# Edge convolution of a graph network: rows gathered two turns ahead, four one-hot slots, four rotating PSUM banks, transposes one group later, node state kept in DRAM

## What is computed

```python
x = norm(x + two hops of normalized neighbour sums of x)
x = norm(x + conv2(leaky_relu(conv1(x))))
x = norm(x + sixteen hops with alpha = 0.1)
x = norm(x + gcn(relu(graph_norm(gcn(x)))))

def _egnn_conv(x, src, dst, edge_attr, W_msg, W_edge, W_root, b):
    msg = x[src] @ W_msg + edge_attr @ W_edge
    agg = jax.ops.segment_max(msg, dst, num_segments=x.shape[0])
    agg = jnp.where(jnp.isneginf(agg), 0.0, agg)
    return agg + x @ W_root + b
```

## Time and profile before

| | us |
|---|---|
| three runs: lowest, median, highest | 2440.36, 2442.22, 2445.31 |
| the profiled execution | 2427.74 |
| its span, first to last instruction | 2425.9 |
| busy: PE, DVE, POOL, ACT | 1989.3, 1248.0, 717.9, 637.2 |
| convolution turns, start of turn 0 to start of turn 25 | 457.52 and 457.16 |
| mean granted clock of PE | 0.931 |

### The profile page before, as it was taken

One profiled execution on the slowest core, in us unless ns is written; L12 is line 12 of the kernel. 1 busy time (PEld: TensorE's weight loads), 2 busy tenths in 40 slices (PEclk: granted clock), 3 DMA queues, 4 the chain that ended last, 5 costly groups with the idle time before them and its releaser, 6 DMA issues. The chain is left out here.

```text
span 2425.9 us, 55088 instructions
## 1 busy us (share of the span) xinstructions
PE 1989.3 (82%) x22874; PEld 1903.6 (78%) x22874; DVE 1248.0 (51%) x3350; ACT 637.2 (26%) x1659; POOL 717.9 (30%) x681
## 2 busy tenths in 40 slices
PE   4587468888888358888888369999999999999877
PEld 3587467787777357877877259999999999999767
DVE  7934446666656336666656454444444444445435
ACT  5832212212211112112112123323333333332231
POOL 4512146656656535566655510000000000000000
PEclk9988789999999679999999679999999999999879
DMA  2023236656655336566656300000000000000000
GB/s 71 1 82 103 83 80 137 136 128 137 137 122 136 92 78 131 125 138 139 132 129 134 94 6 2 2 2 2 2 1 2 2 2 2 2 2 2 3 3 21
DMA packets 223177, 157.62 MB, mean 65 GB/s; under 512 B 147494, under 2 KB 208581, under 8 KB 222679
## 3 DMA queue, kind: packets, MB, share of 16 engines
q1 hardware_dynamic: 90841, 80.91, 12.9%
q0 software_dynamic: 22064, 32.18, 7.9%
q10 hardware_dynamic: 110024, 41.02, 6.2%
HBM read 99.40 MB, written 54.55 MB: 63 GB/s over the span
## 5 line engine op out<-in xcount | busy, mean ns | idle before, releaser
L757 PE MATMUL l_ps<-l_u,counts 125*128 125x192 f16 x11250 | 940.4, 247 | 77.8 <-DVE l_u L800 65.1
L757 PEld LDWEIGHTS l_ps<-l_u,counts 125*128 125x128 f16 x11250 | 935.3, 98 | 82.9 <-issue 64.8
L1119 PE MATMUL c_taken<-y,c_hot 125*128 125x192 f16 x6500 | 601.6, 252 | 174.4 <-issue 74.8
L1119 PEld LDWEIGHTS c_taken<-y,c_hot 125*128 125x128 f16 x6500 | 551.5, 100 | 206.9 <-issue 86.9
L1089 POOL DMA_INDIRECT c_gathered<-messages,idx_all x572 | 567.8, 993 | 397.4 <-PE c_msg L1109 246.1
L1167 DVE TENSOR_SCALAR c_hot<-c_offset_srcs 125x640 f16<-125x640 f16 x1300 | 339.6, 327 | 262.7 <-PE c_taken L1119 187.7
L1177 DVE TENSOR_TENSOR_SCAN c_scanned<-c_mask,c_scanned,c_msg 96x512 f32<-96x512 bf16 x208 | 264.2, 1270 | 127.9 <-remote 101.9
L820 DVE SCALAR_TENSOR_TENSOR l_uf<-l_ps,l_cf,l_wide 125x96 f32<-125x96 f32 x400 | 127.2, 318 | 329.1 <-ACT l_wide L776 329.1
L1231 ACT ACTIVATE c_back<-c_tr 128x384 f32<-128x384 f32 x208 | 103.1, 496 | 625.9 <-PE c_tr L1129 361.9
L776 ACT ACTIVATE l_wide<-l_ps,l_cl 125x96 f32<-125x96 f32 x400 | 136.0, 341 | 306.8 <-PE l_ps L757 306.8
L782 ACT ACTIVATE l_u<-l_uf 125x96 f16<-125x96 f32 x400 | 113.2, 283 | 265.3 <-DVE l_uf L824 254.3
(11 more groups left out here) (236 smaller groups left out, 1143.9 us busy)
## 6 DMA issues: line engine op xcount, KB each, us to landing
running_max<-c_back ACTq DMA_DIRECT2D x208, 192.0 KB
c_attr<-attr_halves SPq DMA_DIRECT2D x412, 64.0 KB
c_mask<-segment_mask SPq DMA_DIRECT2D x206, 96.0 KB
c_gathered<-messages,idx_all POOLq DMA_INDIRECT x572
c_srcs<-sources SPq DMA_DIRECT2D x50, 156.2 KB
l0a_raw<-in_ea_t SPq DMA_DIRECT2D x25, 265.6 KB
attr_halves<-l0a_hi SPq DMA_DIRECT2D x25, 132.8 KB
attr_halves<-l0a_lo SPq DMA_DIRECT2D x25, 132.8 KB
```

Source lines behind the costliest of these rows:

```text
L757: last = pe.matmul(ps[:, t % HB, 0:2 * F], at[:, k, t * P:t * P + 128], u[hop % 2][:, k, :], start=(k == 0), stop=(k == T - 1))
L1119: last = pe.matmul(acc[:, j // 2, j % 2 * (2 * F):(j % 2 + 1) * (2 * F)], hot[:, h % 2 * HALF + k, j * ET:(j + 1) * ET], y[:, t, :], start ...
```

## The change

1. **Gathered rows double-buffered.** `gathered` holds 11 tiles for each of two turns; the taken tiles have their own buffer. POOL's gathers for turn i wait for the messages of turn i-2; those of turns 0 and 1 wait for nothing.
2. **Four one-hot slots.** Eight chunks of 3 blocks (the last has 4) in four slots. DVE refills a slot after the chunk four earlier.
3. **Four rotating banks** for the takes. Turn i uses banks 3i, 3i+1, 3i+2 modulo 4. ACT evacuates and signals each bank on its own; the first and the last chunk of a turn go bank by bank.
4. **Turn-back one group later.** PE: messages 0; chunks 0, 1; turn-back 3 of turn i-1; messages 1; chunks 2, 3; turn-back 0; messages 2; chunks 4, 5; turn-back 1; messages 3; chunks 6, 7; turn-back 2. `evacuate` comes before `send_back` 2 on ACT.
5. **State parked in DRAM.** SP stores `x_state` to `xs_d` at the end of the first two hops, and the next stage begins when the store has landed; SBUF is then free for the buffers above. `conv_result` loads it back, behind the root term on SP's queue, and DVE waits for it before its first use.
6. **Layout of `scan_d`.** Four tiles of a row side by side: stores of 1536 bytes in place of 4 x 384. `end_idx` is worked out for that by seven small DVE operations on 125 x 25 elements, at the start of the first convolution (`ends=True`).
7. `keys`, the hops' `u0` and the rows `y` share one buffer, and sources are loaded a turn earlier.

The diff, cut to what the text speaks of:

```diff
-CHUNKS = (range(0, 5), range(5, 9), range(9, 13), range(13, 17), range(17, 21), range(21, 25))
+CHUNKS = tuple(range(3 * h, 3 * h + 3) for h in range(7)) + (range(21, 25),)
 NC = len(CHUNKS)
-RING = 2 * max(len(r) for r in CHUNKS)
+SLOTS = (0, 3, 6, 9)
+RING = 13
+ACCS = 4
...
+        y = rows16[0:P, :, :]
+        with ExitStack() as s1:
+            xs = s1.enter_context(nc.sbuf_tensor("x_state", [P, T, F], F32))
+            build_counts(ctx, src, dst, xs, x)
+            with ExitStack() as st:
+                hs = hop_state(ctx, st, "l0", teleports=False)
+                hops(ctx, "l0", hs, xs, 1.0, 0.0, 2, norm=xs, out=xs_d, halves=AttrHalves(ctx, st, "l0a"))
+            node_product(ctx, "c1w", xs, "W1_msg", "W1_root", "b1", y16=y)
...
+        edge_conv(ctx, "c1", "W1_edge", y, ends=True)
...
+        edge_conv(ctx, "c2", "W2_edge", y)
+        xs = keep("x_state_back", [P, T, F], F32)
         with ExitStack() as st:
             c2 = st.enter_context(nc.sbuf_tensor("c2", [P, T, F], F32))
-            conv_result(ctx, "c2r", c2, xs)
+            conv_result(ctx, "c2r", c2, xs, xs_d)
...
-        gat = sb("gathered", [ET, IT, 2 * F], F16)
+        gat = sb("gathered", [ET, 2, FROM_POOL, 2 * F], F16)
+        tak = sb("evacuated", [ET, TAKEN, 2 * F], F16)
...
-        acc = st.enter_context(nc.psum_tensor(f"{tag}_taken", [128, NB, BANK], F32))
+        acc = st.enter_context(nc.psum_tensor(f"{tag}_taken", [128, ACCS, BANK], F32))
...
-        scan_v = c["scan_d"].rearrange("(g j p) f -> g p j f", j=GT, p=ET)
+        s_ch = sem(f"{tag}_ch")
+        scan_v = c["scan_d"].rearrange("(g p j) f -> g p j f", j=GT, p=ET)
...
+                load_srcs(1, TE)
                 for i in range(N_IT):
-                    if i < last_it:
-                        load_srcs(i + 1, LEFT_TAKEN if i + 1 == last_it else TE)
+                    if i + 2 < N_IT:
+                        load_srcs(i + 2, LEFT_TAKEN if i + 2 == last_it else TE)
...
                 for i in range(N_IT):
                     for g, tiles in enumerate(by_dma):
-                        pool.wait_ge(s_msg, i * GT + g + 1)
+                        if i >= 2:
+                            pool.wait_ge(s_msg, (i - 1) * GT + g + 1)
                         for j in tiles:
                             pool.indirect_dma_start(
-                                out=gat[:, j, :], out_offset=None, in_=c["y_d"],
+                                out=gat[:, i % 2, j, :], out_offset=None, in_=c["y_d"],
                                 in_offset=bass.IndirectOffsetOnAxis(ap=idx_all[:, i * IT + j:i * IT + j + 1], axis=0),
-                            ).then_inc(s_gat[g], 16)
+                            ).then_inc(s_gat[i % 2][g], 16)
...
                 def take(i, h):
-                    if h == 0:
-                        pe.wait_ge(s_evac, i + 1)
                     pe.wait_ge(s_hot, i * NC + h + 1)
-                    for k, t in enumerate(CHUNKS[h]):
-                        for j in range(TAKEN):
-                            last = pe.matmul(acc[:, j // 2, j % 2 * (2 * F):(j % 2 + 1) * (2 * F)],
-                                             hot[:, h % 2 * HALF + k, j * ET:(j + 1) * ET], y[:, t, :],
-                                             start=(t == 0 and j % 2 == 0), stop=(t == T - 1), skip_group_check=True)
-                    last.then_inc(s_took, 1)
+                    chunk = CHUNKS[h]
+                    slot = SLOTS[h % len(SLOTS)]
+                    def one(k, j):
+                        t = chunk[k]
+                        return pe.matmul(acc[:, (NB * i + j // 2) % ACCS, j % 2 * (2 * F):(j % 2 + 1) * (2 * F)],
+                                         hot[:, slot + k, j * ET:(j + 1) * ET], y[:, t, :],
+                                         start=(t == 0 and j % 2 == 0), stop=(t == T - 1), skip_group_check=True)
+                    if 0 < h < NC - 1:
+                        for k in range(len(chunk)):
+                            for j in range(TAKEN):
+                                last = one(k, j)
+                    else:
+                        for b in range(NB):
+                            if h == 0 and b == 0 and i >= 2:
+                                pe.wait_ge(s_evac, NB * (i - 1))
+                            if h == 0 and b > 0 and i >= 1:
+                                pe.wait_ge(s_evac, NB * (i - 1) + b)
+                            for j in range(2 * b, min(2 * b + 2, TAKEN)):
+                                for k in range(len(chunk)):
+                                    last = one(k, j)
+                            if h == NC - 1:
+                                last.then_inc(s_pair, 1)
+                    if h < NC - 1:
+                        last.then_inc(s_took, 1)
...
-                def body(i, more):
+                def takes(i, *chunks):
+                    if i < N_IT:
+                        for h in chunks:
+                            take(i, h)
+                pe.wait_ge(s_we, 2)
+                takes(0, *range(NC))
+                for i in range(N_IT):
                     messages(i, 0)
-                    if more:
-                        take(i + 1, 0)
-                        take(i + 1, 1)
+                    takes(i + 1, 0, 1)
+                    if i:
+                        turn_back(i - 1, 3)
                     messages(i, 1)
+                    takes(i + 1, 2, 3)
                     turn_back(i, 0)
-                    if more:
-                        take(i + 1, 2)
-                        take(i + 1, 3)
                     messages(i, 2)
+                    takes(i + 1, 4, 5)
                     turn_back(i, 1)
                     messages(i, 3)
-                    if more:
-                        take(i + 1, 4)
+                    takes(i + 1, 6, 7)
                     turn_back(i, 2)
-                    if more:
-                        take(i + 1, 5)
-                    turn_back(i, 3)
-                pe.wait_ge(s_we, 2)
-                pe.sem_inc(s_evac, 1)
-                for h in range(NC):
-                    take(0, h)
-                for i in range(N_IT):
-                    body(i, i < last_it)
+                turn_back(last_it, 3)
...
+                def one_hots(i, *chunks):
+                    for h in chunks if i < N_IT else ():
+                        v.wait_ge(s_off, i + 2)
+                        if h >= len(SLOTS):
+                            v.wait_ge(s_took, i * (NC - 1) + h - len(SLOTS) + 1)
+                        elif i and h < len(SLOTS) - 1:
+                            v.wait_ge(s_took, (i - 1) * (NC - 1) + h + len(SLOTS) + 1)
+                        elif i:
+                            v.wait_ge(s_pair, i * NB)
+                        for k, t in enumerate(CHUNKS[h]):
+                            last = v.tensor_scalar(hot[:, SLOTS[h % len(SLOTS)] + k, :], off[:, :], float(t * P - SRC_MID), None, ALU.is_equal)
+                        last.then_inc(s_hot, 1)
...
+                if ends:
+                    ch = Chain(v, s_ch)
...
+                    v.scalar_tensor_tensor(c["end_idx"][:, :], tile, 1.0 - GW, end, ALU.mult, ALU.add)
...
+                one_hots(0, *range(NC))
+                one_hots(1, 0, 1, 2, 3)
                 for i in range(N_IT):
-                    body(i, i < last_it, i < last_it - 1)
+                    scan(i, 0)
+                    one_hots(i + 1, 4, 5)
+                    scan(i, 1)
+                    one_hots(i + 1, 6, 7)
+                    scan(i, 2)
+                    one_hots(i + 2, 0, 1)
+                    scan(i, 3)
+                    one_hots(i + 2, 2, 3)
...
-                    act.wait_ge(s_took, i * NC + NC)
                     act.wait_ge(s_msg, i * GT + GT)
                     for b in range(NB):
                         n = min(2, TAKEN - 2 * b)
-                        last = act.activation(gat[:, FROM_POOL + 2 * b:FROM_POOL + 2 * b + n, :],
-                                              acc[:, b, 0:n * 2 * F].rearrange("p (j f) -> p j f", f=2 * F), ACT.Copy)
-                    last.then_inc(s_evac, 1)
+                        act.wait_ge(s_pair, NB * i + b + 1)
+                        act.activation(tak[:, 2 * b:2 * b + n, :],
+                                       acc[:, (NB * i + b) % ACCS, 0:n * 2 * F].rearrange("p (j f) -> p j f", f=2 * F),
+                                       ACT.Copy).then_inc(s_evac, 1)
...
+                    if i:
+                        send_back(i - 1, 3)
+                    send_back(i, 0)
+                    if i + 2 < N_IT:
+                        act.wait_ge(s_hot, (i + 2) * NC)
+                        offset_srcs(i + 2)
+                    send_back(i, 1)
+                    if i < last_it:
+                        evacuate(i + 1)
+                    send_back(i, 2)
+                send_back(last_it, 3)
...
                 conv.sync(sp)
```

(3 more changed lines are left out.)

105 lines of the change are left out of this document (34 added, 71 removed).

## The result

| | before | after |
|---|---|---|
| median of the runs, us | 2441.29 (2439.29 to 2445.31, 4 runs) | 2548.03 (2537.39 to 2551.9, 4 runs) |
| the profiled execution | 2427.74 | 2548.67 |
| its span | 2425.9 | 2546.8 |
| busy PE, DVE, POOL, ACT | 1989.3, 1248.0, 717.9, 637.2 | 2052.4, 1257.9, 711.0, 645.0 |

The ratio is 1.0428, with an interval of 1.0394 to 1.0462. The forecast was 2499 us, in a range of 2360 to 2560, with 0.67 for slower. The direction and the place were right; the turns cost far more than I said, and so did the parking.

A forecast was written before the change was run, and what follows sets the result against it. PE bounds the hops; in turns, its signals are also held during POOL's back-to-back gathers. Starts +28.6, turns +25, parking +10.5 and tail -7 took 2427.7 to 2484.8; 14.5 more for the median gave 2499 us, range 2360 to 2560.

The forecast's parts named there:

- What bounds the kernel: In turns, PE's 14.4 us of work in 18.3, with the rest lost to the evacuation wait and the hold.
- The hold: While POOL issues gathers back to back, PE's signals from about 2 us in wait until about 1 us after.
- A, the starts: Start of each convolution: 22 gathers in one run instead of 11, 14.3 us later each, +28.6 in all.
- B, the turns: 50 turns: evacuation wait goes, PE halts earlier in gather runs, more runs merge; +25 us, bounds -100 to +60.
- The merged runs: Turns where POOL runs through two groups' gathers: one in seven or so costs 3.5 us more, +0.5 a turn.
- The plain turn: Turn with gather runs of 4, 4, 3: 14.4 work + 3.4 + 0.5 halts = 18.3 us, as before.
- C, the parking: Store ending the first hops +3.5 us, fetch behind the root term in conv_result +7; together +10.5.
- D: Small parts (index operations, longer store packets, evacuate order, earlier sources, shared buffers): 0 us, bounds 0 to 3.
- E: Tail: the last two turns of each convolution have no gathers beside them, -3.5 us each, -7 in all.
- Double-buffering pays: Rival in the turns: PE still meets four-gather runs late, turn 16.3 us, 2374 us in all; chance 0.15.
- PE gets further: Rival in the turns: PE runs 32 takes further past a held signal, turn near 15.9, 2354 us; chance 0.10.

The follow-up runs named there:

- gated run: Changed kernel with POOL's waits as before the change (gathers wait for the previous turn's messages), undoing double-buffering alone; 2520.53 us (one run).
- the parking in the better order: Changed kernel, SP storing four fifths of the state before the last attribute halves and fetching root term and state fifth by fifth; 2534.99 us (one run).

## Why the prediction was right, and where it was short

**What bounds the kernel: right.** The hold decides the sign. It goes with the spacing of the gathers: the table above has a border between 1.4 and 1.50 us in the quiet start and between 1.50 and 1.57 in the turns. That fits the 1.44 a gather, read from one idle time of DVE, as the rate at which a backlog goes; the backlog itself is not seen.

**A, the starts: right.** +13.4 and +13.0 against 14.3 each. The gated run gives it back, and more.

**B, the turns: right in kind, short by 51 us** (+69 with the tail against +18). The 48 turns with gathers grew by 76 us, which lies outside B's own bound of +60, and the turn is 19.6 and 19.8 on average where I had given 18 to 19. The whole stayed in the range all the same, as it had been drawn wide. Three things in it:

- The merged runs. I took one turn in seven, each 3.5 us above a plain turn of 18.3; one in three merged, which I had as the bound. They took 21.55, 3.25 above 18.3, so the price was about right and the number was not: 16 x 3.25 = 52 us instead of 25.
- The plain turn. It took 19.07 instead of 18.3: 32 x 0.77 = 25 us. **The term that was mis-sized is PE's 14.4 us of work, not its halts.** In the 19 plain turns at full clock PE is busy for 15.4 and idle for 3.55, where I had 14.4 and 3.9; before, plain turns at full clock had 15.1 and 2.8. A matmul that PE does alone in a hold counts 0.32, in a stream 0.083, so a turn with halts has more busy time than its matmuls have in a stream. PE's idle time in all 32 plain turns is 3.1: 0.5 in the first run, not 1.7, 1.9 in the second, and 0.6 in the third.
- The clock, which I had noted at 0.98 and left at that. In plain turns it is no large part: the 13 with the clock down are busy for 1.3 us more and idle for 1.1 less, and take 0.2 more. In the merged turns it is: among those of 8 and 3, the two at full clock took 19.6 and the eight others 21.3. The kernel before had such turns too, 9 plain ones at 19.3 where 33 at full clock took 17.9. If the six turns of 4 and 7 lost as much as those of 8 and 3, the clock took 26 us now and 13 before: an estimate of 13 of the 76 us. Why one turn with halts loses its clock and the next does not, no run shows.

Why PE runs into the hold earlier, I put on the chunks' signals, 15 takes apart. Chunks of 20 gave 19 us of the turns back, not the whole. The other candidates, the turn-back's place and the missing wait for the evacuation, which kept PE idle while POOL was idle too, were not tried apart.

**C, the parking: short by 9.** The store was priced from the program's last store, 4.6 us. That one moves a fifth of the state; here all five fifths were queued behind the attribute halves on SP, and the queue moved 1.2 MB in about 12 us. By the idle time before the node product the store costs some 12 to 13 us, where I had 3.5. I had the rate at hand, since the fetch's row gave it, and used it for the fetch alone, which came out at +8.2 against +7.

**D: right, E: right** (the last turns are 14.3 and 14.4, where both were 17.8 before: 3.5 and 3.4 less).

**The rivals.** "Double-buffering pays" fell: the gated kernel has the same turns. "PE gets further" fell: at the start PE did 51 takes, 21 past the signal of chunk 1 that came late, and then one at a time, so a queue of 64, as the Trainium skill has it on the page "TensorE: Matmul & The Clock Gate", section "Architectural detail: the array is 16x 32x32, not 1x 128x128", did not carry it through the hold. No run here measures the queue itself.

A faster version exists, though, by 0.6%. It is the change with its gathers slowed by 0.3 us each and the parking in the better order.

## What to carry to other kernels

Where PE, DVE, ACT and SP all stop at once and resume within half a us of each other, look for the engine that was busy all the while: here POOL's gathers, and the cure was to issue them more slowly. Deeper buffering lets an engine run longer without a pause, so ask before it what a long run does to the others. And when PE is halted again and again, don't add up its work from its best stretches: PE was busy for 15.4 us in a turn whose work I had summed as 14.4. A lower clock behind a halt doesn't simply add either: in the turn shown it cost 1.6 us of work, and the turn was 0.4 us longer, since PE was idle for less of it.

## What the runs showed of the hardware that I had not expected

- Row gathers of 128 rows issued every 1.25 us held PE's signals for 1.42 us a gather in a run of 22, and for 12.0 us in a run of 8 in the turns (396.62 to 408.6, 1.50 a gather). Every 1.58 us or slower they hold next to nothing. DVE's own signals passed meanwhile (PE began its takes at 324.58 on one of them), and one of PE's came through in the middle of the run of 22 (339.49). What the backlog is, no run shows; it is neither the bytes (192 or 384 a row, the same) nor the DMA engines (19% busy).
- During a hold PE doesn't stop altogether. It does single matmuls 0.7, 1.4, 2.1 or 2.8 us apart (340.11, 342.93, 343.66, 345.76, 347.16), each near a multiple of 0.7.
- A pause of the wrong length costs more than none: at 1.39 us the changed kernel took 2596, at 1.25 us 2548, at 1.63 us 2481.
